# Fused transformer layers with two expert stages: norm of the last layer moved behind the return of the rows, 23 and 29 tiles

## The chip, the cores and the metric

The program runs on one core of a Trainium2 chip. The metric is device time in microseconds (us) of one execution; the median of three runs before the change is 597.67 us (596.51 to 597.98). The core has a matmul engine (TensorE, PE in the rows; PEld is its weight load), VectorE (DVE), ScalarE (ACT), GpSimd (POOL) and SyncE (SP), which run their own instruction queues in order and wait for each other through semaphores. DMA transfers are issued here by SP and by POOL.

## What is computed

Four blocks over x of shape (4, 512, 128), each followed by a layer norm of residual plus block, all in float32. Only the last one is touched by the change, with the tile counts of both expert blocks:

```
x = _layernorm(x + attention_0(x))
x = _layernorm(x + experts_0(x))      # 8 experts, F = 512, SiLU, top 1
x = _layernorm(x + recurrence_1(x))
x = _layernorm(x + experts_1(x))      # 14 experts, F = 256, GELU, top 1
return x

# experts_1
assignments = argmax(x @ router_w)             # one expert for each of the 2048 rows
weights = softmax(x @ router_w)[assignments]
hid = gelu(x @ w1[e] + b1[e]);  y = hid @ w2[e] + b2[e]
out = y[assigned] * weights
# _layernorm(v): (v - mean(v)) / sqrt(var(v) + 1e-5), over the 128 values of a row
```

## The kernel before

The 2048 rows lie as 16 tiles of 128 rows (four batches of four tiles). Each expert stage works in three steps. GpSimd scatters the rows with indirect DMAs into DRAM, one region of 2048 rows for each expert (L519). VectorE works out on the core which region and offset each "slot tile" of 128 rows comes from (`tabulate`, L1193 on), since the counts per expert are data. Then the slot tiles are worked through in a ring of three. The number of slot tiles is fixed at build time: the most that any split of 2048 rows over E experts can need is (2048 + 127 E) // 128, which is 23 for 8 experts and 29 for 14; `slot_tiles` rounds it up to a multiple of the ring, to 24 and 30. A slot tile past the used ones holds zero rows with an index that the scatter drops.

For each slot tile m of the second expert stage:

- SP reads the tile's offset and loads its 128 rows of 130 values (the row, its index, its router weight) from the region (L470, L473).
- TensorE transposes it (L1010), ScalarE copies it out of PSUM (`turned`, L805), TensorE makes the two hidden chunks (L1018), ScalarE applies GELU (`raised`, L812), TensorE makes the result (L1027).
- VectorE fetches the expert's weights, 642 columns, into the ring (L1393), adds bias (`summed`, L1423), forms statistics of the tile before (`spread`, L1413), multiplies by the router weight and adds the residual (L1428), and combines mean and variance of the tile before (`moments`, L1417). The matmuls of a tile wait for its weight copy.
- GpSimd (`outputs`) takes tiles in groups of three (the last two alone): variance plus epsilon (L507), power -0.5 (L510), minus mean (L623), times scale (L627); after group k it sends the three tiles of group k - 2.
- ScalarE (`normed`, L817) applies scale and shift to tile m - 7, in its queue between the copies and GELUs of tiles m and m - 1, and waits for the group's shift there.
- GpSimd sends a normed tile with one indirect DMA straight to the rows of the output (L616). SP waits at the end for all 30.

```
            for m in range(NT1 + NORM_LAG):
                if m < NT1:
                    turned(m)
                if 1 <= m <= NT1:
                    raised(m - 1)
                if m >= NORM_LAG:
                    normed(m - NORM_LAG)
```

The first expert stage has no norm behind it in the tile loop: VectorE adds the bias, GpSimd scatters the tile into the DRAM tensor `returned_0` (L605), and when all have landed SP loads the rows back in token order with four DMAs of 256 KB (L482); VectorE goes on from there (L1472). Its ScalarE code is six tiles written out and a hardware loop over the rest, three tiles an iteration.

## Time and profile before

| what | value |
|---|---|
| runs | 596.51, 597.67, 597.98 us, median 597.67 |
| the profiled execution | 597.33 us, of which its span (first to last instruction) 595.5 us |
| busy of the span | PE 78%, weight load 55%, VectorE 59%, ScalarE 46%, GpSimd 46% |
| last region of the program, from 588.0 us on | no engine busy |

The profiled execution lies 1.8 us above its own span and 0.3 us below the median. The program has five stretches: attention up to about 320 us, first expert stage to 377 us, recurrence to 503 us, second expert stage to 588 us, and the end. The span is cut in 40 slices in the page, of 14.9 us each; the last three show VectorE at 4, 0 and 0 tenths and GpSimd at 7, 7 and 3:

```profile
DVE  2545666767776777667344666475865656484600
POOL 4323255428654573440212455433445645167773
```

### The profile page before, as it was taken

The page shows a single profiled execution, that of the slowest core. Times are in us where ns is not written, and L with a number is a line of the kernel's source. Part 1 is how long each engine was busy: PE and PEld are TensorE (multiplying, and loading weights), DVE is VectorE, ACT ScalarE, POOL GpSimd, SP SyncE. Part 2 cuts the span into 40 slices and gives each one's busy share as a digit, 9 for nine tenths or more (in the row PEclk, how much of TensorE's full clock was granted, in tenths as well). Part 3 has the DMA queues.
Part 4 walks back from the last instruction along what each step waited for, and adds up shares of the span by engine and source line. Part 5 has one row for each costly group of instructions (what it writes and reads, how often), then busy time and mean ns, then how long its engine had stood idle before and what let it go on. Part 6 is the DMA issues. An engine that isn't in the chain of part 4 may idle for free. (4 is left out here: it accounts for less than half of the span.)

```text
span 595.5 us, 9976 instructions
## 1 busy us (share of the span) xinstructions
PE 465.0 (78%) x3101; PEld 327.2 (55%) x3101; DVE 352.9 (59%) x878; ACT 274.3 (46%) x570; POOL 272.3 (46%) x310
## 2 busy tenths in 40 slices
PE   3888999999999999999666999189797962786600
PEld 3465566565666567666443999134554651665500
DVE  2545666767776777667344666475865656484600
ACT  1043556665666565767310555174462210576510
POOL 4323255428654573440212455433445645167773
PEclk9955999999999999999967999679899985698955
DMA  8999999999920000000211320630000001221100
GB/s 325 179 171 171 164 348 187 193 201 185 190 48 14 2 1 2 19 2 1 81 53 40 81 58 21 215 165 0 0 2 0 19 18 36 56 69 36 36 15 0
DMA packets 65171, 50.73 MB, mean 85 GB/s; under 512 B 3110, under 2 KB 63277, under 8 KB 64480
## 3 DMA queue, kind: packets, MB, share of 16 engines
q1 hardware_dynamic: 62368, 45.87, 39.4%
q0 software_dynamic: 2752, 4.24, 2.1%
q8 instruction: 26, 0.43, 0.3%
q14 instruction: 25, 0.20, 0.1%
HBM read 20.37 MB, written 31.15 MB: 87 GB/s over the span
## 5 line engine op out<-in xcount | busy, mean ns | idle before, releaser
L697 ACT ACTIVATE arena<-banks 128x512 f32<-128x512 f32 x128 | 76.4, 597 | 99.1 <-PE banks L900 98.9
L900 PE MATMUL banks<-ca,work 128*128 128x128 f32 x512 | 86.3, 293 | 17.9 <-ACT arena L697 15.5
L690 ACT ACTIVATE work<-banks,nmax 128x512 f32<-128x512 f32 x128 | 80.7, 686 | 14.2 <-DVE nmax L1273 14.0
L900 PEld LDWEIGHTS banks<-ca,work 128*128 128x128 f32 x512 | 56.2, 146 | 55.7 <-issue 44.2
L1273 DVE TENSOR_REDUCE nmax<-banks 128x2 f32<-128x1024 f32 x64 | 78.4, 1224 | 2.2
L884 PE MATMUL banks<-arena 32*128 32x512 f32 (+3 forms) x256 | 63.2, 454 | 0.0
L873 PEld LDWEIGHTS banks<-arena 32*128 32x128 f32 x256 | 43.2, 193 | 34.3 <-issue 23.7
L873 PE MATMUL banks<-arena 32*128 32x128 f32 x256 | 57.4, 305 | 1.5 <-DVE corr L1356 0.9
L1018 PE MATMUL banks<-t,arena 128*128 128x128 f32 x312 | 50.8, 303 | 4.0 <-ACT t L805 2.4
L1261 DVE COPY_PREDICATED banks<-ca,banks 128x256 f32<-128x256 uint32 x64 | 27.3, 426 | 44.7 <-PE banks L873 44.6
L1018 PEld LDWEIGHTS banks<-t,arena 128*128 128x128 f32 x312 | 43.7, 210 | 7.1 <-issue 4.0
L1027 PE MATMUL banks<-arena,work 128*128 128x128 f32 x312 | 46.4, 286 | 0.9 <-ACT work L812 0.6
L879 PE MATMUL banks<-arena 32*128 32x128 f32 (+2 forms) x192 | 46.2, 419 | 0.0
L1073 PE MATMUL banks<-arena 128*128 128x512 f32 x96 | 43.0, 596 | 1.2 <-POOL arena L669 1.2
L736 ACT ACTIVATE work<-banks,arena 128x128 f32<-128x128 f32 x96 | 27.4, 368 | 32.9 <-PE banks L1018 32.9
L1027 PEld LDWEIGHTS banks<-arena,work 128*128 128x128 f32 x312 | 41.5, 201 | 1.6 <-ACT work L812 1.1
L913 PE MATMUL banks<-arena 128*32 128x256 f32 x512 | 40.9, 394 | 0.0
L605 POOL DMA_INDIRECT returned<-work,arena x24 | 24.0, 998 | 33.1 <-DVE work L1406 19.4
L519 POOL DMA_INDIRECT regions<-xc,pos x16 | 16.4, 1026 | 48.7 <-DVE pos L1183 44.9
L884 PEld LDWEIGHTS banks<-arena 32*128 32x128 f32 x256 | 37.6, 194 | 1.3
L572 POOL TENSOR_TENSOR arena<-ca,corr 128x512 f32<-128x512 f32 x32 | 33.1, 1041 | 8.7 <-DVE nmax L1273 7.3
L1393 DVE COPY arena<-arena 128x642 f32 (+1 forms) x54 | 32.6, 603 | 6.6 <-DVE work L1406 4.5
(212 smaller groups left out, 852.6 us busy)
## 6 DMA issues: line engine op xcount, KB each, us to landing
regions<-zeros SPq DMA_DIRECT2D x15, 1040.0 KB, 18.1
regions<-zeros SPq DMA_DIRECT2D x9, 1032.0 KB, 20.3
arena<-wp_in SPq DMA_DIRECT2D x1, 4624.0 KB, 28.3
arena<-wp_in SPq DMA_DIRECT2D x1, 4494.0 KB, 15.9
arena<-ct_in SPq DMA_DIRECT2D x1, 2048.0 KB, 10.3
arena<-regions SPq DMA_DIRECT2D x30, 65.0 KB, 1.8
arena<-cb_in SPq DMA_DIRECT2D x1, 1667.0 KB, 8.2
arena<-regions SPq DMA_DIRECT2D x24, 64.5 KB, 1.9
```

Of the source, the lines that this page charges most:

```text
L572: eng.tensor_tensor(delta[:, i, :, :], A("ident").unsqueeze(1).broadcast_to([P, HG, P]), corr[:, b % 2, i, g * HG:(g + 1) * HG].unsqueeze( ...
L690: eng.activation(prob[:, r, :], bank[r], ACT.Exp, bias=nmax[:, s % 2, jj:jj + 1]).then_inc(s_exp, 1)
L697: eng.activation(probT[:, v % 2, j0 + jj, :, i % 2 * P:(i % 2 + 1) * P], PT.rearrange("p (t q) -> p t q", t=TB), ACT.Copy).then_inc(s_pTs, 1)
L873: return eng.matmul(DA[:, jj * P:(jj + 1) * P], qa[rows, r, g, mine], ka[rows, r, g, mine], start=True, stop=True)
L879: eng.matmul(bank[2 * (s % 2) + jj][:, 0:split], qa[rows, r, g, mine], ka[rows, r, g, 0:split], start=True, stop=True)
L884: eng.matmul(bank[2 * (s % 2) + jj][:, split:S], qb[rows, r, g, mine], kb[rows, r, g, split:S], start=True, stop=True)
L900: mm = eng.transpose(PT[:, t * P:(t + 1) * P], prob[:, 2 * (s % 2) + jj, t * P:(t + 1) * P], ident)
L913: mm = eng.matmul(CTX[HP * j:HP * (j + 1), 2 * P * hh:2 * P * (hh + 1)], vv[:, b % 2, t, h * HP:(h + 1) * HP], probT[:, v % 2, j, t, :], s ...
L1018: mm = eng.matmul(bank[r][:, c * P:(c + 1) * P], wbuf[:, r, c * P:(c + 1) * P], xTs[:, r, :], start=True, stop=True)
L1027: mm = eng.matmul(bank[3 + r][:, 0:D], hT[:, r, c * P:(c + 1) * P], wbuf[:, r, F + c * D:F + (c + 1) * D], start=(c == 0), stop=(c == CH - 1))
L1073: mm = eng.matmul(bank[4 + v % 2], R(name, k * INNER + c * P, P), uu[:, r, k, :], start=(k == 0), stop=(k == NC - 1))
L1273: eng.tensor_reduce(nmax[:, s % 2, :], pair, AX.X, ALU.max, negate=True).then_inc(count(s_fixed), 1)
```

## The change

The tile counts become 23 and 29. In the second expert stage the norm leaves the tile loop. A tile's rows, before the norm, now have mean and variance as two more columns (`moments` writes them beside the row), and GpSimd scatters the 130-wide rows in token order into a new DRAM tensor `returned_1`, with nothing else in its queue. When all 29 have landed, SP loads them back in four DMAs of four tiles. ScalarE takes the root of variance plus epsilon of a batch's four tiles, VectorE the reciprocal and the shift, and the norm is split, two tiles of a batch on VectorE and two on ScalarE; SP stores each pair with a plain DMA, eight in all. A table load for the root (with a dummy root behind it) stands at the end of ScalarE's tile loop. The first stage's ScalarE loop is written out.

```
-NORM_LAG = 7
+BY_DVE = 2
 def slot_tiles(experts):
-    most = (B * S + experts * (P - 1)) // P
-    return -(-most // RING) * RING
+    return (B * S + experts * (P - 1)) // P
...
+    sums = nc.dram_tensor("returned_1", (B * S, DW1), F32, kind="Internal").ap()
-        y1 = arena2[:, 0:NT1 * D].rearrange("p (m d) -> p m d", m=NT1)
+        y1 = arena2[:, 0:NT1 * DW1].rearrange("p (m d) -> p m d", m=NT1)
...
             expert_rows(1, E1, NT1)
-            eng.wait_ge(s_store, 16 * NT1)
+            eng.wait_ge(s_sent, 16 * NT1)
+            for b in range(B):
+                eng.dma_start(xbw[:, b * TB:(b + 1) * TB, :],
+                              sums[b * S:(b + 1) * S, :].rearrange("(t p) d -> p t d", p=P)).then_inc(s_back1[b], 16)
+            for b in range(B):
+                for k, s_half in enumerate((s_fin_v, s_fin_a)):
+                    at = slice(b * TB + k * BY_DVE, (b + 1) * TB if k else b * TB + BY_DVE)
+                    eng.wait_ge(s_half, (b + 1) * (TB - BY_DVE if k else BY_DVE))
+                    eng.dma_start(out_view[:, at, :], xa[:, at, :]).then_inc(s_store, 16)
+            eng.wait_ge(s_store, 2 * 16 * B)
...
+            eng.memset(eps1[:, :], 1e-5).then_inc(s_set, 1)
...
-            def outputs():
...
+            def sums_back():
+                for m in range(NT1):
                     eng.wait_ge(s_xload[1][m % LOADS], 16 * (m // LOADS + 1))
-                    eng.wait_ge(s_norm1, m + 1)
-                    eng.indirect_dma_start(out_rows, bass.IndirectOffsetOnAxis(ap=xt[:, m, D:D + 1].bitcast(I32), axis=0),
+                    eng.wait_ge(s_var1, m + 1)
+                    eng.indirect_dma_start(sums[:, :], bass.IndirectOffsetOnAxis(ap=xt[:, m, D:D + 1].bitcast(I32), axis=0),
                                            y1[:, m, :], None, bounds_check=B * S - 1, oob_is_err=False)\
-                       .then_inc(s_store, 16)
...
-                for m in range(2 * RING):
+                for m in range(nt):
                     tile(m, m % RING, m < RING)
-                with eng.Fori(2, nt // RING) as it:
-                    for r in range(RING):
-                        tile(it * RING + r, r, False)
...
-            for m in range(NT1 + NORM_LAG):
+            for m in range(NT1 + 1):
                 if m < NT1:
                     turned(m)
-                if 1 <= m <= NT1:
+                if m >= 1:
                     raised(m - 1)
-                if m >= NORM_LAG:
-                    normed(m - NORM_LAG)
+            eng.activation(few[:, 0:1], eps1[:, :], ACT.Sqrt).then_inc(s_outa, 1)
+            for b in range(B + 1):
+                if b < B:
+                    eng.wait_ge(s_back1[b], 16)
+                    eng.activation(scale1[:, b * TB:(b + 1) * TB], xbw[:, b * TB:(b + 1) * TB, D + 1], ACT.Sqrt,
+                                   bias=eps1[:, :]).then_inc(s_root, 1)
+                if b >= 1:
+                    eng.wait_ge(s_scale1, 2 * b)
+                    for t in range((b - 1) * TB + BY_DVE, b * TB):
+                        eng.activation(xa[:, t, :], xb[:, t, :], ACT.Identity, bias=shift1[:, t:t + 1],
+                                       scale=scale1[:, t:t + 1]).then_inc(s_fin_a, 1)
...
-                    eng.bn_aggr(mv1[:, m, :], st1[:, m, :]).then_inc(s_var1, 1)
+                    eng.bn_aggr(y1[:, m, D:D + 2], st1[:, m, :]).then_inc(s_var1, 1)
...
             experts(1, NT1, F1, WW1, wp1)
+            for b in range(B):
+                tiles = slice(b * TB, (b + 1) * TB)
+                eng.wait_ge(s_root, b + 1)
+                eng.reciprocal(scale1[:, tiles], scale1[:, tiles]).then_inc(s_scale1, 1)
+                eng.wait_ge(s_scale1, 2 * b + 1)
+                eng.scalar_tensor_tensor(out=shift1[:, tiles], in0=xbw[:, tiles, D], scalar=-1.0, in1=scale1[:, tiles],
+                                         op0=ALU.mult, op1=ALU.mult).then_inc(s_scale1, 1)
+                for t in range(b * TB, b * TB + BY_DVE):
+                    eng.tensor_scalar(xa[:, t, :], xb[:, t, :], xbw[:, t, D:D + 1], scale1[:, t:t + 1],
+                                      ALU.subtract, ALU.mult).then_inc(s_fin_v, 1)
```

How it moves instructions. GpSimd's queue in the second expert stage, before (one group of three tiles and its sends; each such row is one instruction, "x3" three):

```order
L510 TENSOR_TENSOR scale<-scale,half 128x3
L623 TENSOR_SCALAR shift<-mv 128x3
L627 TENSOR_TENSOR shift<-shift,scale 128x3
L616 DMA out<-arena 2048x128 x3
L507 TENSOR_SCALAR scale<-mv 128x1
```

The four small operations of a group stand between the sends of one group and the next. Now, from the last scatters into the regions (L531) to the end of GpSimd's queue:

```order
L531 DMA regions<-xb,pos 30720x130 x4
L519 TENSOR_SCALAR rstda<-mva 128x4
L522 TENSOR_TENSOR rstda<-rstda,half 128x4
L531 DMA regions<-xb,pos 30720x130 x8
L626 DMA returned<-arena 2048x130 x29
L194 UNCONDITIONAL_BRANCH
```

Between the 29 sends nothing is left. ScalarE's queue at the end of the tile loop, before:

```order
L805 ACTIVATE t<-banks 128x128
L812 ACTIVATE work<-banks,arena 128x128 x2
L817 ACTIVATE arena<-arena,shift,scale 128x128
L812 ACTIVATE work<-banks,arena 128x128 x2
L817 ACTIVATE arena<-arena,shift,scale 128x128 x7
L194 UNCONDITIONAL_BRANCH
```

The norm (L817) of an earlier tile stands between the copy and the GELUs of each two tiles. The same place now:

```order
L797 ACTIVATE t<-banks 128x128
L804 ACTIVATE work<-banks,arena 128x128 x4
L813 ACT_TABLE_LOAD
L813 ACTIVATE few<-eps 128x1
L817 ACTIVATE scale<-xb,eps 128x4 x2
L822 ACTIVATE xa<-xb,shift,scale 128x128 x2
L817 ACTIVATE scale<-xb,eps 128x4
L822 ACTIVATE xa<-xb,shift,scale 128x128 x2
L817 ACTIVATE scale<-xb,eps 128x4
L822 ACTIVATE xa<-xb,shift,scale 128x128 x4
L194 UNCONDITIONAL_BRANCH
```

The norm activation between two tiles' GELUs is gone. The root of batch b + 1 stands ahead of the norm of batch b, and no second table load follows.

## Rows read from the trace of the kernel before

**Rows 1.** Waits, 528 to 566 us: who for whom, us in total, times, longest
```profile
ACT arena L817 <- POOL shift L627: 12.5, 6, 3.1
```

**Rows 2.** Timeline, second expert stage, GpSimd: start us, us, engine, line, operation
```profile
540.69 0.19 POOL L507 TENSOR_SCALAR scale<-mv 128x3 f32<-128x3 f32 x1
542.95 1.25 POOL L616 DMA_INDIRECT out<-arena  x1 [0.60 <-ACT arena L817]
544.51 0.98 POOL L616 DMA_INDIRECT out<-arena  x1 [0.30 <-issue]
...
546.84 0.19 POOL L507 TENSOR_SCALAR scale<-mv 128x3 f32<-128x3 f32 x1
```

**Rows 3.** Timeline, the end of the second expert stage, and the waits of SP's queue
```profile
565.02 0.18 DVE L1417 BATCH_NORM_AGGREGATE mv<-st 128x2 f32<-128x6 f32 x1
587.23 0.97 POOL L616 DMA_INDIRECT out<-arena  x1 [0.30 <-issue]
...
SPq L194 <- PEq L194: 6.0, 1, 6.0
```

**Rows 4.** Timeline, VectorE between 516 and 535 us
```profile
516.13 0.18 DVE L1417 BATCH_NORM_AGGREGATE mv<-st 128x2 f32<-128x6 f32 x1
...
517.58 0.46 DVE L1393 COPY arena<-arena 128x642 f32 x1
518.18 0.29 DVE L1423 TENSOR_TENSOR arena<-banks,arena 128x128 f32<-128x128 f32 x1
...
534.64 0.29 DVE L1423 TENSOR_TENSOR arena<-banks,arena 128x128 f32<-128x128 f32 x1
```

**Rows 5.** Timeline, the last hidden matmuls, and SP's loads of slot tiles
```profile
561.74 0.71 PE L1018 MATMUL banks<-t,arena 128*128 128x128 f32 x4 [2.38 <-ACT t L805]
...
506.49 23.93 SPq L473 DMA_DIRECT2D arena<-regions  x22
```

**Rows 6.** The first stage's returns: its sends, then the timeline of its end
```profile
L605 POOL DMA_INDIRECT returned<-work,arena x24: 980/982/1353, 330.5 to 375.1; - x24
...
374.00 0.29 DVE L1406 TENSOR_TENSOR work<-banks,arena 128x128 f32<-128x128 f32 x1 [1.21 <-PE banks L1027]
377.29 2.03 SPq L482 DMA_DIRECT2D xa<-returned  x4
380.21 1.14 DVE L1472 SCALAR_TENSOR_TENSOR xc<-xa,sm,xb 128x128 f32<-128x128 f32 x4 [5.58 <-DMA xa<-returned]
```

**Rows 7.** Windows: us, busy of PE, PEld, DVE, ACT, POOL, granted PE clock, DMA share, GB/s
```profile
328.00:374.00 46.00, 45.62 (x392) 44.80 (x390) 28.60 (x65) 27.52 (x93) 22.37 (x23) 1.00 0.19 52
506.00:513.50 7.50, 4.09 (x16) 3.50 (x17) 0.00 (x0) 3.15 (x8) 0.00 (x0) 0.50 0.20 47
520.00:531.00 11.00, 10.20 (x74) 8.43 (x73) 9.79 (x42) 9.17 (x32) 5.81 (x12) 1.00 0.26 61
```

**Rows 8.** DMAs to landing: SP's loads of returned rows (L482), then issues by kind
```profile
DMA to landing us min/median/max: 2.9/3.9/5.8
...
out<-arena POOLq DMA_INDIRECT x30, 2.2
...
regions<-xb,pos POOLq DMA_INDIRECT x16, 2.3
```

**Rows 9.** Timeline: durations of the kinds that the change adds, and of a table load
```profile
567.02 1.26 ACT L817 ACTIVATE arena<-arena,shift,scale 128x128 f32<-128x128 f32 x3 [3.53 <-POOL shift L627]
...
385.35 1.12 DVE L1464 TENSOR_SCALAR z<-xc,mva,rstda 128x128 f32<-128x128 f32 x4
...
498.37 0.18 DVE L1550 RECIPROCAL xb<-sm 128x4 f32<-128x4 f32 x1
...
510.32 1.28 ACT L812 ACT_TABLE_LOAD   x1
```

**Rows 10.** Timeline: VectorE's bias additions of tiles 0 and 1, at the low clock
```profile
513.55 0.29 DVE L1423 TENSOR_TENSOR arena<-banks,arena 128x128 f32<-128x128 f32 x1 [8.49 <-PE banks L1027]
...
515.47 0.29 DVE L1423 TENSOR_TENSOR arena<-banks,arena 128x128 f32<-128x128 f32 x1 [0.83 <-PE banks L1027]
```

54 lines of the change are left out of this document (19 added, 35 removed).

## Prediction
> **What bounds the kernel now.** I read the timeline of the last hundred microseconds first, then the waits there, then the windows for the clock. Up to the second expert stage nothing but tile counts, a 0.1 us memset and the form of one ScalarE loop changes, so this is where the case is decided. The reader is to see that the stage is not bound by its arithmetic. GpSimd's queue sets the pace: from one group's first small operation to the next group's it is 546.84 - 540.69 = 6.15 us for three tiles, 2.05 us a tile, of which the three sends take 546.84 - 542.95 = 3.9 us and the small operations with the pauses around them the rest [rows 2]. ScalarE stands still for GpSimd's shift, 12.5 us between 528 and 566 us in six waits [rows 1], and since the norm sits in ScalarE's queue ahead of the next tile's copy, TensorE and VectorE stand too. Where GpSimd isn't yet in the way the loop is faster: VectorE's bias additions of tiles 3 and 15 stand at 518.18 and 534.64 us, 16.46 us for 12 tiles, 1.37 us a tile, with VectorE busy 9.79 of 11.0 us in that stretch [rows 4, 7]. And after VectorE's last statistics at 565.20 us the program goes on for 30.3 us of the 595.5 us span: GpSimd works off its backlog until 588.20 us, the last send lands, and 6.0 us of program end follow [rows 3].
>
> **The change, part by part.** All on the time scale of the profiled execution (span 595.5, time 597.33 us).
>
> *First stage, 24 to 23 tiles.* TensorE is busy 45.62 of 46.00 us there and the sends go from 330.5 to 375.1 us in 23 steps, 1.94 us each [rows 6, 7]. One tile less is 1.94 us off the path, since the returns, and all behind them, wait for the last send. Writing out ScalarE's loop: ScalarE is busy 27.5 of 46 us and waits for TensorE; nothing. The memset and the small table instructions (29 in place of 30 columns): nothing, they stand beside DMA waits.
>
> *Second stage, the loop.* Removed: 11 groups of four GpSimd operations, 30 norm activations, one tile. Each engine's load then is: VectorE as before, 1.37 us a tile; GpSimd one send, 1.28 us when one follows another (0.98 and 0.30) [rows 2]; SP one load in 23.93 / 22 = 1.09 us [rows 5]. VectorE becomes the bound, with SP's loads hidden ahead of it and GpSimd just hidden behind it. The start doesn't move (tile 3 at 518.18 us). Tile 26's bias addition comes at 518.18 + 23 x 1.37 = 549.7 us; the copy of the last tile's weights ends 0.14 us before that (it ends at 518.04 ahead of 518.18) [rows 4], at 549.55; the last hidden matmuls wait for it alone, I put 0.1 us; and from these to the end of the last statistics it is 565.20 - 561.74 = 3.46 us [rows 3, 5]. That gives 553.1 us in place of 565.2 us: 12.1 us off.
>
> *Second stage, the tail.* In place of the 30.3 us:
> - Last statistics to SP's first load of the returned rows: the first stage has the same chain, 374.29 to 377.29 us, 3.0 us [rows 6]. It holds only if GpSimd has no backlog.
> - First load issued to landed: 377.29 to 380.21 us, 2.9 us [rows 6].
> - Four batches through ScalarE. The loads there landed 2.9 to 5.8 us after issue, with issues 0.5 us apart, and the last of them shared the DMA engines with the load of the second stage's weights, issued right behind it [rows 8]. So the last lands 1.5 us (the issues alone) to 4.4 us (5.8 + 1.5 - 2.9) after the first; I take 2.7, 0.9 us a load, as there is no weight load here. ScalarE's order is root 0, root 1, norm 0, root 2, norm 1, root 3, norm 2, norm 3. It starts its chain with the second landing, 0.9 us, and then has three roots and eight norm activations; three of these take 1.26 us in a row, 0.42 each [rows 9]; a root of 4 columns I put at 0.3 with its wait (no row has one; between the 0.18 of the reciprocal and a norm's 0.42, both without a wait). Together 0.9 + 0.9 + 3.4 = 5.2, and 0.1 for a wait: 5.3 us. VectorE needs less, 0.2 + 0.2 and two operations of 0.28 a batch [rows 9], beside it. Bounds: 4.8 with landings 0.5 us apart; 6.5 if the last landing comes 4.4 us late and root, reciprocal, shift and four norms follow it.
> - The last store of 128 KB: no row shows a plain store. The scatters of 64 KB land in 2.2 and 2.3 us, the load of 256 KB in 2.9 [rows 8]; I take 2.4 with the issue, between 2.1 and 3.5.
> - The end: 6.0 us [rows 3].
>
> Sum 3.0 + 2.9 + 5.3 + 2.4 + 6.0 = 19.6 us, 10.7 less than 30.3. The table load of 1.28 us [rows 9] stands in ScalarE's queue while the returns travel (5.9 us), so it is hidden; without that cover it would cost its 1.3 us.
>
> Total: 1.9 + 12.1 + 10.7 = 24.7 us off, span 570.8, time 572.6 us in the profiled execution. The median stands 0.34 us above that execution: **573.0 us**.
>
> The returned rows are 520 bytes long in place of 512. What bears on it: scatters of 520-byte rows land in 2.3 us and of 512-byte rows in 2.2 us [rows 8], so I charge nothing. The Trainium skill (DMA: Bandwidth & Descriptors, section How a descriptor splits into AXI transactions) speaks against the change: a descriptor that doesn't start at a multiple of 256 bytes is split into more transactions, 25 beats in place of 18 in its example of 576 bytes. By that rule, an estimate from the page, the loads would be spaced nearer 1.3 than 0.9 us and the sum would be about 574. The rows here show no such difference for scatters, and none shows it for loads.
>
> **The rivals.**
>
> *A, the sends don't keep pace.* In the first stage each send starts 0.84 us after VectorE's result (374.29 to 375.13, "375.1") and takes 0.98 [rows 6]. If each of the 29 sends pays both, 1.82 us, GpSimd is the bound again: from the first statistics (516.31 - 1.94 = 514.4 us) 28 x 1.82 = 51.0 to the start of the last wait and 0.84 to its send, 566.2 us, in place of 551.2 + 0.84 = 552.0. That is 14.2 us more, 587. For it: in the first stage all sends looked like that. Against: a send that is already due follows after 0.30 us, 1.28 us in all, with VectorE busy [rows 2], so one that falls behind catches up. The Trainium skill (GPSIMD Engine Reference, section 1. Specifications) says that GpSimd shares its SBUF interfaces with VectorE and contends with two-input and two-port operations; by that page VectorE's work in the loop would slow the sends, which would feed this rival. The rows speak against that: 0.98 us and 0.30 us before it for a send in the middle of VectorE's work, 0.97 and 0.30 at the end, when VectorE is idle [rows 2, 3].
>
> *B, the clock stays low.* At 506 to 513.5 us TensorE has half clock (0.50, the level of 1.2 GHz) after a long pause, and tiles 0 and 1 are 1.92 us apart; from 520 us it has 1.00 [rows 7, 10]. Should it stay low, 25 tiles x 0.55 = 13.8 us more: 587. Against it: the loop before reaches 1.00 in the same work, and the new loop only has fewer pauses.
>
> *C, slower: the scatters drain one by one.* If the DMA queue of GpSimd takes a scatter of 520-byte rows only when the one before has landed, 29 x 2.3 us [rows 8] from 515.2 us ends at 581.9 us, in place of 554.2 for SP's first load: 27.7 us more, 600.7 us. It decides from 2.26 us a scatter on. Against it: sends are issued 1.28 us apart, each landing in 2.1 to 2.3 us, so two are under way together [rows 2, 8].
>
> *D, the change saves less in the tail*: landings, semaphores and SP's eight store issues at 0.5 us add up to 5 us more than summed, 578.
>
> **How the numbers follow.** Forecast 0.74, D 0.08 (inside the range), A 0.08, B 0.05, C 0.03, something else that leaves the time where it is 0.02. The low end takes 0.3 in place of 0.84 us for the last send, ScalarE's 4.8, the store's 2.1 and a pace of 1.33 us, 0.5 + 0.5 + 0.3 + 1.0 = 2.3 us less, and 1.2 us for the spread of the runs (597.67 to 596.51): 569.5. The high end takes 1.2 for ScalarE, 1.1 for the store and 2.3 for a pace of 1.46, 577.6, or D, and with the spread 579.5. A measurement of this kernel tells 0.3% (1.8 us) from no change. Faster 0.96, same 0.01, slower 0.03.
>
> **What would show it.** Right: no wait of ScalarE for GpSimd in the second stage; VectorE's bias additions 1.37 us apart to the end; last statistics at 551 us; 29 sends about 1.37 us apart with the last starting under 1 us after the last statistics; SP's first load at 554, its landing at 557, the last norm at 562, the last store landed at 565. Wrong: sends 1.8 us apart (A), a granted clock of 0.50 behind 515 us (B), landing times that grow from send to send (C), a table load between root and norm, or over 6 us between the first landing and the last store's issue (D).

## The result, and the profile after

| | before | changed |
|---|---|---|
| median of 4 runs each, beside each other | 597.23 us (596.51 to 597.98) | 564.62 us (558.62 to 567.04) |
| ratio, with its 95% interval | | 0.942 (0.9335 to 0.9505) |
| the profiled execution, its span | 597.33, 595.5 us | 567.04, 565.1 us |
| busy of the span: PE, VectorE, ScalarE, GpSimd | 78, 59, 46, 46% | 81, 63, 47, 44% |

The kernel is 32.6 us faster in the median. The forecast said 24.7 us (573.0 us), and its range went down to 569.5 us, 5 us above the result: right in direction, too small in size. Executions of one kernel lie up to 14 us apart here, the shorter ones with a higher mean granted clock of TensorE (the kernel before, in later runs, 588 to 591 us at 0.902 and above, 596 to 603 us at 0.888 and below), and the ratios here and below leave out the executions over 1.5% above the fastest of their kernel, so they can differ a little from those of the medians.

Where the clock differs is ahead of anything that the change touches. Between 30 and 60 us TensorE is granted 0.50 to 0.53 in eleven of the fourteen profiles of this study and 0.89 to 0.91 in three. The changed kernel's profile (0.51) and that of the kernel with its sends held back (0.91), described below, run the same instructions on VectorE up to the second expert stage's statistics, and reach the first of these at 512.5 and at 503.2 us. Of the 32.6 us some 2 come from this: the kernel before's four executions, 596.5 to 598.0 us, all have the lower clock by their times, the changed kernel's have 566.6 and 567.0 us with the lower one (means 0.902 and 0.905), 562.6 and 558.6 us with a higher one (0.913 and 0.921). With the lower clock in both it is 30 us, and the two profiled executions, 0.52 and 0.51 between 30 and 60 us, are 30.3 us apart.

The profiled run splits at two instants that both kernels have, the first and the last of VectorE's statistics in the second expert stage:

| stretch | before | changed | difference | forecast |
|---|---|---|---|---|
| start of the program to VectorE's first bias addition there | 513.55 | 509.95 | -3.60 | -1.94 |
| first to last statistics | 48.9 | 37.0 | -11.9 | with the tile count -12.1 |
| end of the last statistics to the end of the span | 30.3 | 15.4 | -14.9 | -10.7 |

The loop first. The waits of the changed kernel between 513 and 548 us (who for whom, us in total, times, longest) in place of [rows 1]:

```profile
ACT work L804 <- PE banks L1015: 13.8, 25, 0.9
POOL returned L626 <- DVE arena L1414: 12.7, 1, 12.7
POOL returned L626 <- issue: 9.1, 25, 0.7
...
DVE arena L1420 <- PE banks L1024: 0.5, 1, 0.5
```

ScalarE waits only for TensorE, 0.9 us at the most; no wait of it for GpSimd is left. VectorE waits for TensorE once, 0.5 us. VectorE's timeline at the start of the loop (start us, us, engine, line, operation), to hold against [rows 4, 10]:

```profile
509.95 0.29 DVE L1420 TENSOR_TENSOR arena<-banks,arena 128x128 f32<-128x128 f32 x1 [8.45 <-PE banks L1024]
511.87 0.29 DVE L1420 TENSOR_TENSOR arena<-banks,arena 128x128 f32<-128x128 f32 x1 [0.84 <-PE banks L1024]
513.23 0.29 DVE L1420 TENSOR_TENSOR arena<-banks,arena 128x128 f32<-128x128 f32 x1
514.58 0.29 DVE L1420 TENSOR_TENSOR arena<-banks,arena 128x128 f32<-128x128 f32 x1
515.94 0.29 DVE L1420 TENSOR_TENSOR arena<-banks,arena 128x128 f32<-128x128 f32 x1
```

From the second tile on they stand 1.35 to 1.36 us apart (two later steps take 1.54 and 1.71), without an idle gap here, so VectorE is the bound, as forecast (1.37). The windows (us, busy of PE, PEld, DVE, ACT, POOL, granted PE clock, DMA share, GB/s), to hold against [rows 7], show full clock, but don't decide the bound: VectorE is busy 28.26 of 32 us and TensorE 28.41. What decides it is who waits, and the run with the bias on TensorE below.

```profile
240.00:320.00 80.00, 63.53 (x484) 41.11 (x480) 44.96 (x110) 37.42 (x63) 22.29 (x28) 0.94 0.09 31
...
516.00:548.00 32.00, 28.41 (x207) 23.77 (x208) 28.26 (x117) 19.18 (x69) 23.38 (x24) 1.00 0.29 71
```

The first line bears on the other 1.66 us of the start: over the same 80 us of attention, which the change doesn't touch, this execution has a granted clock of 0.94 and the one before 0.89. The experiments come back to it.

Then the end. Timeline of the changed kernel from the third last statistics on, in place of [rows 3]:

```profile
548.11 0.17 DVE L1414 BATCH_NORM_AGGREGATE arena<-st 128x2 f32<-128x6 f32 x1
...
549.08 0.17 DVE L1414 BATCH_NORM_AGGREGATE arena<-st 128x2 f32<-128x6 f32 x1
...
549.42 0.98 POOL L626 DMA_INDIRECT returned<-arena  x1 [0.38 <-DVE arena L1414]
549.53 0.18 DVE L1414 BATCH_NORM_AGGREGATE arena<-st 128x2 f32<-128x6 f32 x1
550.70 0.98 POOL L626 DMA_INDIRECT returned<-arena  x1 [0.30 <-issue]
551.98 0.98 POOL L626 DMA_INDIRECT returned<-arena  x1 [0.30 <-issue]
554.14 2.03 SPq L491 DMA_DIRECT2D xb<-returned  x4
557.08 0.30 ACT L817 ACTIVATE scale<-xb,eps 128x4 f32<-128x4 f32 x1 [7.95 <-DMA xb<-returned]
...
558.33 4.98 SPq L497 DMA_DIRECT2D out<-xa  x8
...
560.90 1.63 ACT L822 ACTIVATE xa<-xb,shift,scale 128x128 f32<-128x128 f32 x4
```

And what SP waits for last, with the drain of GpSimd's queue that ends a program (duration in ns three times, first and last start):

```profile
L194 POOLq DRAIN  x1: 9428/9428/9428, 550.5 to 550.5; - x1
```

```profile
SPq L194 <- DMA out<-xa: 1.4, 1, 1.4
```

The wait of 6.0 us at the program's end [rows 3] has gone; 0.2 us of it is left. In the kernel before, GpSimd's drain stands at 585.5 us:

```profile
L194 POOLq DRAIN  x1: 9757/9757/9757, 585.5 to 585.5; - x1
```

It ends at 585.5 + 9.76 = 595.3 us, the end of the program and 8.1 us after the last send's start at 587.23. In the changed kernel it ends at 550.5 + 9.43 = 559.9 us, 7.9 us after 551.98, but now 5 us ahead of the end, beside loads and norms. That is an observation on two traces; the experiments ask whether it is the cause.

### The profile page after: what moved, and what is told of

Same layout as the page of the kernel before. It is cut to its first block and busy times, and to the rows that moved or that the text cites. A ratio compares the mean times of both kernels' runs of the same rounds, so it can differ in the third digit from the quotient of the medians.

```text
span 565.1 us, 9780 instructions
## 1 busy us (share of the span) xinstructions
PE 457.9 (81%) x3075; PEld 319.9 (57%) x3075; DVE 354.3 (63%) x886; ACT 266.6 (47%) x547; POOL 250.3 (44%) x261
## 5 line engine op out<-in xcount | busy, mean ns | idle before, releaser
L897 PE MATMUL banks<-ca,work 128*128 128x128 f32 x512 | 86.5, 294 | 17.9 <-ACT arena L692 15.5
L1015 PE MATMUL banks<-t,arena 128*128 128x128 f32 x300 | 47.6, 297 | 3.7 <-ACT t L797 1.0
L876 PE MATMUL banks<-arena 32*128 32x128 f32 (+2 forms) x192 | 46.3, 420 | 0.0
L1015 PEld LDWEIGHTS banks<-t,arena 128*128 128x128 f32 x300 | 40.7, 205 | 8.7 <-issue 7.2
L1024 PE MATMUL banks<-arena,work 128*128 128x128 f32 x300 | 43.4, 281 | 0.9 <-ACT work L804 0.5
L731 ACT ACTIVATE work<-banks,arena 128x128 f32<-128x128 f32 x92 | 26.2, 368 | 32.2 <-PE banks L1015 31.1
L1024 PEld LDWEIGHTS banks<-arena,work 128*128 128x128 f32 x300 | 38.8, 197 | 1.5 <-ACT work L804 1.0
L626 POOL DMA_INDIRECT returned<-arena x29 | 29.4, 1012 | 22.7 <-DVE arena L1414 13.0
L531 POOL DMA_INDIRECT regions<-xc,pos x16 | 16.4, 1024 | 48.1 <-issue 30.2
L617 POOL DMA_INDIRECT returned<-work,arena x23 | 22.6, 983 | 32.5 <-DVE work L1403 30.9
## 6 DMA issues: line engine op xcount, KB each, us to landing
arena<-wp_in SPq DMA_DIRECT2D x1, 4494.0 KB, 15.4
```

Of the source, the lines that this page charges most:

```text
L876: eng.matmul(bank[2 * (s % 2) + jj][:, 0:split], qa[rows, r, g, mine], ka[rows, r, g, 0:split], start=True, stop=True)
L897: mm = eng.transpose(PT[:, t * P:(t + 1) * P], prob[:, 2 * (s % 2) + jj, t * P:(t + 1) * P], ident)
L1015: mm = eng.matmul(bank[r][:, c * P:(c + 1) * P], wbuf[:, r, c * P:(c + 1) * P], xTs[:, r, :], start=True, stop=True)
L1024: mm = eng.matmul(bank[3 + r][:, 0:D], hT[:, r, c * P:(c + 1) * P], wbuf[:, r, F + c * D:F + (c + 1) * D], start=(c == 0), stop=(c == CH - 1))
```

## The experiments

They ran in four groups, each on a chip of its own; kernels of one group share their runs of the kernel before.

### The drain

The changed kernel once more, unaltered:

> The changed kernel once more, for its spread. Four runs so far lie between 558.6 and 567.0 us, far wider than the 1.5 us of the kernel before, and its profiled run reached tile 3 of the second expert stage 3.60 us earlier than before where one tile of the first stage accounts for 1.94. Theory N (the rest is the granted TensorE clock between 240 and 330 us, 0.94 against 0.89, which changes from run to run): the median of five comes out within 2 us of 564.6, and in the new profile the 1.6 us are of another size or gone. Theory L (the rest comes with the written-out ScalarE loop or another layout in memory): tile 3 comes 3.6 us earlier than before again, within 0.3 us.

The tile counts and ScalarE's written-out loop alone; statistics, norm and sends as in the kernel before:

```diff
 def slot_tiles(experts):
-    most = (B * S + experts * (P - 1)) // P
-    return -(-most // RING) * RING
+    return (B * S + experts * (P - 1)) // P
```

> The kernel before with 23 and 29 tiles and the first stage's ScalarE loop written out, the norm where it was. Theory N: 1.94 us off in the first stage and 2.05 us (GpSimd's pace of a tile) in the second, 593.2 us against 597.2. Theory L: 1.6 us more than that off, 591.6. In both the end of the program comes 8.0 us after GpSimd's last send starts, 6.0 us after that send has landed.

The norm behind the returns alone, with the rounding to 24 and 30 tiles and ScalarE's loop kept:

> The changed kernel with 24 and 30 tiles and the hardware loop on ScalarE in the first stage, so only the norm moved. Theory N: 1.94 us and one tile of the new pace, 1.36 us, more than the changed kernel: 567.9 us where that has 564.6. Theory L: 1.6 us more again, 569.5. Bias additions of the second stage 1.36 us apart in both, and the last send 2.3 us behind the last statistics, since the last three statistics come faster (0.97 and 0.46 us apart) than sends can follow (1.28).

The changed kernel with one more send at the very end, to rows that nobody reads:

```diff
             eng.wait_ge(s_store, 2 * 16 * B)
+            eng.wait_ge(s_spare, 16)
 ...
+                eng.wait_ge(s_fin_v, B * BY_DVE)
+                eng.indirect_dma_start(spare[:, :], bass.IndirectOffsetOnAxis(ap=xt[:, 0, D:D + 1].bitcast(I32), axis=0),
+                                       y1[:, 0, :], None, bounds_check=B * S - 1, oob_is_err=False)\
+                   .then_inc(s_spare, 16)
```

> The changed kernel plus one more indirect send on GpSimd, of tile 0's rows into a spare DRAM tensor, once VectorE has done its last norm (about 561.9 us in the profiled run); SP waits for its landing too. Theory G (the 6.0 us after the last landing in the kernel before were GpSimd's drain, which ends 8.0 us after its last send starts, and the change hid it by sending early): last send starts about 562.8, the drain ends at 570.8 and the span with it, 5.8 us more than the changed kernel. Rival H (the 6.0 us belonged to the end of that program in some other way, such as more instructions or semaphores to leave): the send lands by 565.0 us, about when the last store does, and the time goes up by under 0.5 us.

Measured, beside 596.79 us before:

| kernel | median us | ratio, 95% interval | span of its profile |
|---|---|---|---|
| changed, again | 571.12 | 0.9629 (0.9533 to 0.9725) | 574.7 |
| tile counts alone | 591.02 | 0.994 (0.9876 to 1.0005) | 581.5 |
| norm behind the returns alone | 581.29 | 0.9822 (0.9752 to 0.9892) | 581.1 |
| changed, with a late send | 583.64 | 0.9873 (0.9829 to 0.9918) | 584.1 |

The late send decides. Its timeline, waits of SP and drain:

```profile
565.09 0.98 POOL L629 DMA_INDIRECT returned<-arena  x1 [0.30 <-issue]
...
575.89 0.98 POOL L633 DMA_INDIRECT spare<-arena  x1 [9.83 <-DVE xa L1571]
```

```profile
SPq L195 <- PEq L195: 5.5, 1, 5.5
```

```profile
L195 POOLq DRAIN  x1: 8223/8223/8223, 575.7 to 575.7; - x1
```

All rows of the output are computed by then, the stores are about to land (the changed kernel's program ends 2.6 us behind its last norm), and still the program ends at 584.1 us, 8.2 us after the spare send's start; the drain ends at 575.7 + 8.22 = 583.9. From the last statistics to the end it takes 21.3 us, where the changed kernel beside it takes 15.2: 6.1 us more, with theory G's 5.8 and against rival H's 0.5. The wait of the old end is back with 5.5 us. So the 6.0 us in the kernel before were no fixed end of every program but the rest of GpSimd's drain behind its last indirect send. The drain ends 7.9 to 8.1 us after the start of the last send in all fourteen profiles of this study, both kernels' own among them, wherever that send stands. With the tile counts alone, where GpSimd still sends last, the end is 8.1 us after the last send (573.36 to 581.5) and SP's wait is 5.8 us; with the norm behind the returns alone it is 0.2 us. That part of the gain therefore comes with the norm's new place, not with the tile counts.

How the gain splits between the two parts this group shows only roughly. The tile counts alone are 5.8 us under the kernel before in the median, with an interval that reaches 1; among the executions with the higher clock it is 585.3 us in the median beside 588.8, 3.5 us for the theory's 4. The first to the last statistics take 47.7 us there, the old pace of 1.7 us. The norm behind the returns alone is 15.5 us under it, and 13 us above both of its theories (567.9 and 569.5), with a loop of 49.8 us that has the pauses described below.

The run of the changed kernel brought something neither theory had: 46.3 us from first to last statistics in place of 37.0. More on that below, under the pauses. Of what it asked, the start of the second stage, it says this: the first bias addition comes at 511.0 us here and at 510.0, 512.6 and 511.5 us in the changed kernel's other three profiles, and at 513.6 and 512.2 us in the two of the kernel before. Executions of one kernel differ there by as much as the 1.66 us beyond the one tile, so nothing shows these to be an effect of the change, and theory L's 3.6 us again didn't come (2.6). Theory N's median within 2 us of 564.6 didn't either (571.1), for the pauses.

### Sends beside the loop, and the bound of the loop

This chip showed no pauses. The kernel before and the changed one once more:

> The kernel before once more, for its profile on the chip of the runs beside it. In the last set the changed kernel's second stage took 46.3 us from the first to the last statistics where the run shown with the result took 37.0, with pauses of 1.3 to 2 us about every 5 to 6 us in which VectorE and ScalarE stand and go on within 0.03 us of each other. Theory S (slack): the kernel before has such pauses too, but its loop waits for GpSimd anyway, so they cost it little: first to last statistics within 1.5 us of the 48.9 shown. Rival C (changed code): the pauses come only with the changed kernel, and the kernel before shows no stretch in which VectorE and ScalarE resume together other than behind GpSimd's shift.

> The changed kernel a third time. If the pauses belong to the chip or to the execution, their number here tells: none and the second stage takes 37.0 us from first to last statistics, or as in the last set some six and it takes 45 to 46. The tail is the same in both: last send 2.3 us behind the last statistics, first load 2.2 us behind it, first root 2.9 us later, end of span 15.4 us behind the last statistics.

All 29 sends held back until the last statistics:

```diff
             def sums_back():
+                eng.wait_ge(s_var1, NT1)
```

> The changed kernel with all 29 sends held back until the last statistics are done. Theory P (the sends have a part in the pauses: they write while the loop reads): without sends in the loop no pauses, first to last statistics 37.0 us or less. Rival Q (they belong to TensorE's work, its clock or the loads): the pauses are there as before. In both, 29 sends back to back take 29 x 1.28 = 37.1 us behind the last statistics, about 35 us more than the changed kernel in the same state.

The bias addition given to TensorE, as one more matmul of the bank's sum, and taken from VectorE:

```diff
-                        eng.wait_ge(s_yb[l], m - (RING - 1))
+                        eng.wait_ge((s_yb[0], s_sum1)[l], m - (RING - 1))
+                    if l:
+                        eng.matmul(bank[3 + r][:, 0:D], ident, wbuf[:, r, 2 * F + CH:2 * F + CH + D], start=True, stop=False)
 ...
-                    eng.tensor_tensor(y1[:, m, 0:D], bank[3 + m % RING][:, 0:D], wbuf[:, m % RING, 2 * F + F // P:width],
-                                      ALU.add).then_inc(s_yb[1], 1)
 ...
-                    eng.scalar_tensor_tensor(out=y1[:, m, 0:D], in0=y1[:, m, 0:D], scalar=xt[:, m, D + 1:D + 2],
+                    eng.scalar_tensor_tensor(out=y1[:, m, 0:D], in0=bank[3 + m % RING][:, 0:D], scalar=xt[:, m, D + 1:D + 2],
```

> The changed kernel with the second stage's bias added by TensorE (one more matmul of the identity with the bias columns, 0.11 us) and VectorE reading PSUM once in place of twice (0.21 us less a tile). Theory V (VectorE sets the pace of 1.36 us): where no pauses stand, the pace falls to that of GpSimd's sends, 1.28 us, and the last send starts 2 to 2.6 us earlier behind the first statistics. Rival T (TensorE and the round trip between the engines set it): the pace stays at 1.36 or rises by the 0.11 us of the matmul.

Measured, beside 595.75 us before:

| kernel | median us | ratio, 95% interval | first to last statistics | from there to the end |
|---|---|---|---|---|
| before, again | 596.90 | 1.0049 (0.9993 to 1.0106) | 50.4 | 29.8 |
| changed, a third time | 568.49 | 0.9394 (0.9318 to 0.947) | 37.0 | 15.1 |
| sends held back | 596.97 (592.0 to 601.91) | | 37.0 | 49.8 |
| bias on TensorE | 560.92 | 0.9388 (0.933 to 0.9446) | 34.5 | 15.1 |

The third run of the changed kernel repeats the split of the first within 0.4 us (37.0 and 15.1 against 37.0 and 15.4), so both terms stand. Its six times are 557.0, 561.0 and 568.4 to 570.0 us, the first two with a mean granted clock of 0.92 to 0.93 and the others with 0.90. The ratios of the second and the last line are equal although the medians are 7.6 us apart, because their executions mix the clocks differently; what the bias brings is read from the stretches.

With the sends held back VectorE's loop takes its 37.0 us as ever, and the 28 steps between sends take 36.0 us afterwards:

```profile
540.24 0.18 DVE L1415 BATCH_NORM_AGGREGATE arena<-st 128x2 f32<-128x6 f32 x1
541.21 0.99 POOL L627 DMA_INDIRECT returned<-arena  x1 [49.64 <-DVE arena L1415]
...
577.15 0.98 POOL L627 DMA_INDIRECT returned<-arena  x1 [0.30 <-issue]
```

(577.15 - 541.21) / 28 = 1.28 us, with VectorE idle. The stretch behind the last statistics is 34.7 us longer than the changed kernel's, for an expected 35; the medians are only 28.5 us apart, as the four and six executions mix the clocks differently. Two things follow. The sends cost nothing while they run beside the loop, and they don't slow VectorE: its loop is no faster when GpSimd is silent. And 1.28 us a send is GpSimd's own pace, 0.08 us under VectorE's. What the run was made for, whether the sends have a part in the pauses, it can't say, as no kernel had them on this chip.

The bias on TensorE brings 37.0 - 34.5 = 2.5 us and not 29 times the 0.28 us of the operation taken from VectorE, 8 us. VectorE waits for no send in this loop, so GpSimd can't be what holds its statistics back. TensorE is; its waits, timeline and windows:

```profile
DVE st L1413 <- PE banks L1026: 5.9, 22, 0.6
```

```profile
520.41 0.39 PE L1024 MATMUL banks<-arena,ca 128*128 128x128 f32 x2
520.63 0.61 PE L1026 MATMUL banks<-arena,work 128*128 128x128 f32 x4
```

```profile
514.00:541.00 27.00, 26.89 (x235) 26.29 (x234) 21.44 (x86) 19.09 (x64) 20.57 (x21) 1.00 0.32 82
```

TensorE is busy 26.89 of 27 us, and VectorE waits for it at 22 tiles; the statistics come 1.23 and 1.28 us apart in turn. The added matmul is listed as two and takes 0.22 us (520.41 to 520.63), where 0.11 was expected. So theory V names the bound before (the pace falls from 1.36 us), and rival T's TensorE is the one right behind it. GpSimd is as near: the sends run from 511.5 to 547.5 us, 28 steps of 1.286 us with none but their own 0.3 us between, and the last starts 2.3 us behind the last statistics, as in the changed kernel, so all of the 2.5 us arrive at the end.

### What the tile counts are worth, and what bounds the tail

The changed kernel a fourth time:

> The changed kernel once more, unaltered, as the partner of the next two on the same chip. Theory (differences between its executions come from the start, by the clock that TensorE is granted in 30 to 60 us): times fall on two levels, about 557 to 561 and about 567 to 570 us, and behind the loop's first statistics everything is as before: 36.9 to 37.0 us from the first statistics of the second expert layer to the last, 15.2 to 15.4 us from there to the end of the span. Rival (the loop itself varies, as in the run that took 571.1 us): 45 to 46 us from first to last statistics, with gaps in which VectorE and ScalarE stop together, and times of 570 us and more.

The norm behind the returns alone, again:

```diff
+    most = (B * S + experts * (P - 1)) // P
+    return -(-most // RING) * RING
 ...
-                for m in range(nt):
+                for m in range(2 * RING):
                     tile(m, m % RING, m < RING)
+                with eng.Fori(2, nt // RING) as it:
+                    for r in range(RING):
+                        tile(it * RING + r, r, False)
```

> The root, reciprocal and norm behind the returns alone; the arena's tiles stay 24 and 30 and ScalarE's loop keeps its form. Theory: what the tile counts are worth is one tile of the first layer (1.94 us) and one of the second (1.36 us), so this kernel takes 3.3 us more than the changed kernel beside it (about 568 where that has 564.6), with the last statistics about 38.3 us behind the first ones. Rival (ScalarE's loop, written out by the step, brings something by itself): 4.9 us more than the changed kernel, with 1.6 us more ahead of the second layer's first bias addition than the one tile explains.

The bias on TensorE, and three of a batch's four tiles normed by VectorE:

```diff
-BY_DVE = 2
+BY_DVE = 3
```

> The changed kernel with its bias additions on TensorE (as in the earlier run of that form: 34.6 us from first to last statistics, 15.2 us from there to the end) and with three instead of two of each batch's four tiles normed by VectorE. Theory (ScalarE's chain of roots and norms bounds the stretch behind the last landing): ScalarE has one norm less in each batch, the last norm ends 0.5 to 0.9 us earlier after the last statistics, and the stretch to the end of the span falls from 15.2 to 14.3 to 14.7 us. Rival (the landings of SP's loads and its eight store issues of 0.6 us each bound it): the stretch stays at 15.1 to 15.3 us and the norms only end earlier ahead of stores that wait their turn. What falls the other way: VectorE's third norm comes later than ScalarE's second would have, and the stretch grows by up to 0.5 us.

Measured, beside 597.67 us before (588.91 to 602.89):

| kernel | median us | ratio, 95% interval | first to last statistics | from there to the end |
|---|---|---|---|---|
| changed, fourth time | 568.94 | 0.9634 (0.9574 to 0.9693) | 47.0 | 15.0 |
| norm behind the returns alone | 582.10 | 0.9828 (0.9748 to 0.9907) | 50.5 | 15.0 |
| bias on TensorE, 3 of 4 on VectorE | 575.38 | 0.9662 (0.9579 to 0.9744) | 47.9 | 14.8 |

This chip has the pauses, so the rival on the first kernel held here: 47.0 us, as in the first group. For the bound of the tail the stretch behind the last statistics is clean of them. It came out at 14.8 us, in the gap between the theory's 14.3 to 14.7 and the rival's 15.1. The timeline:

```profile
575.50 0.30 ACT L817 ACTIVATE scale<-xb,eps 128x4 f32<-128x4 f32 x1
...
576.42 0.85 DVE L1564 TENSOR_SCALAR xa<-xb,scale 128x128 f32<-128x128 f32 x3
576.54 0.49 ACT L822 ACTIVATE xa<-xb,shift,scale 128x128 f32<-128x128 f32 x1 [0.35 <-DVE shift L1561]
```

ScalarE is done at 577.03 and VectorE at 577.27 us: both halves now end together, 4.95 us after the first root, where the kernel with the bias on TensorE and two of four takes 5.06 and the changed kernel's profile 5.45. No gain of the new balance is shown: with two of four on VectorE the stretch takes 14.8 to 15.4 us in eight profiles (14.8 with the norm behind the returns alone, first group), so 14.8 lies within what executions differ by. And the bias on TensorE, which took 2.5 us off the loop on the chip before, brings nothing on this one: 47.9 us beside 47.0. Its median is 6.4 us higher, most of which is the clock (three of its six executions have a mean of 0.92, five of the changed kernel's); among those with 0.92 it takes 569.2 to 571.4 us beside 568.2 to 570.3. No version of this study is shown to beat the changed kernel on every chip.

The tile counts are not settled by this. The kernel without them takes 13.2 us more in the median, and 584.0 - 575.6 = 8.4 us more in the profile, where the theory gave 3.3 and the rival 4.9. Of the 8.4 us the first stage has 2.0 (24 sends from 331.5 to 376.1 against 23 from 331.2 to 373.8; the forecast's 1.94), the loop 3.5 (one tile of 1.36 and 2.1 us more of pauses), and 2.7 lie between the stages: from the first stage's last send to the first statistics of the second it has 142.2 us and the changed kernel beside it 139.5, where ten of the other profiles have 140.4 to 141.4. In the first group the medians of the same pair lay 10.2 us apart. So the two tiles themselves are seen with their 3.3 us. The difference of the medians is in good part the clock: of the six executions the kernel without the counts has one with a mean granted clock of 0.917 (574.9 us) and five with 0.894 to 0.903 (579.5 to 585.8), the changed kernel five with 0.918 to 0.921 (568.2 to 570.3) and one with 0.900 (577.5). At like clocks they are some 5 to 6 us apart, and the first group's executions of the kernel without the counts all have the lower clock too. What is left beyond 3.3 us has no cause shown; that the loop of ScalarE, written out by the step, has a part in it is possible and was not tried alone.

### The pauses

On the chips of the first and the third group the second expert stage takes 9 to 13 us more than elsewhere: 46.3 and 47.0 us for the changed kernel's 37.0 from first to last statistics, 45.6 with the late send, 49.8 and 50.5 us with 30 tiles, 47.9 for 34.5 with the bias on TensorE. The timeline of the changed kernel, fourth time:

```profile
517.04 0.97 POOL L626 DMA_INDIRECT returned<-arena  x1 [0.34 <-issue]
...
517.21 0.61 PE L1024 MATMUL banks<-arena,work 128*128 128x128 f32 x4
518.60 0.29 DVE L1420 TENSOR_TENSOR arena<-banks,arena 128x128 f32<-128x128 f32 x1 [2.01 <-PE banks L1024]
518.63 0.28 ACT L797 ACTIVATE t<-banks 128x128 f32<-128x128 f32 x1 [1.62 <-remote]
...
524.51 0.29 DVE L1420 TENSOR_TENSOR arena<-banks,arena 128x128 f32<-128x128 f32 x1 [1.98 <-PE banks L1024]
524.54 0.28 ACT L797 ACTIVATE t<-banks 128x128 f32<-128x128 f32 x1 [1.55 <-PE banks L1007]
```

VectorE and ScalarE, both waiting for TensorE, resume 0.03 us apart, 1.3 to 2.0 us late; in the first of these pauses no compute engine starts anything for about 1 us (up to 518.60). The bias additions with over 1 us of idle time ahead of them are those of these tiles, counted from one:

| kernel | group | tiles |
|---|---|---|
| changed, again | first | 5, 8, 14, 17, 20, 25 |
| norm behind the returns alone | first | 5, 11, 14, 17, 20, 24, 27 |
| changed, with a late send | first | 5, 8, 11, 15, 18, 25 |
| changed, fourth time | third | 5, 8, 12, 15, 21, 25 |
| norm behind the returns alone, again | third | 5, 8, 11, 14, 17, 20, 26 |
| bias on TensorE, 3 of 4 on VectorE | third | 5, 8, 11, 14, 17, 20, 23, 26 |

They come at every third or fourth tile, at nearly the same ones in all six. As the loops also start alike and keep nearly the same pace, this doesn't tell a place in the program from a time since the loop began; a time since the start of the program it isn't, since the loops start up to 5 us apart. The last row is the tile whose result VectorE waits for, as that kernel has no bias addition; TensorE has six matmuls a tile there in place of five, and the tiles are the same, which speaks against a count of TensorE's own instructions.

TensorE isn't alone in it. SyncE stands too, in register instructions that wait for no engine. Their durations (ns, least, median, longest) in the changed kernel, fourth time, and below it in the third, without pauses:

```profile
L475 SPq MOVE arena<-regions x52: 3/29/693, 321.2 to 541.7; - x52
```

```profile
L475 SPq MOVE arena<-regions x52: 29/29/29, 322.8 to 537.3; - x52
```

All seven profiles of the first and the third group have such moves of 0.39 to 0.71 us at the longest, also in the first expert stage, and the other seven none over 0.03 us. The kernel with the tile counts alone is one of the first seven (0.39 us), though its first fifteen statistics stand 1.35 to 1.36 us apart with one step of 1.55, without a pause at tile 5, 8, 11 or 14. So the disturbance of these two chips isn't TensorE's alone, and it is there without the new norm too. Records of 3 ns, a tenth of what the same instruction takes elsewhere, stand beside the long ones, so the recording of the instructions may have a part in it; nothing here tells.

What it costs the comparison can be said. With the higher clock the kernel before takes 588 to 591 us on all three chips, pauses or not; the changed kernel takes 557.0 and 561.0 us on the chip without them and, with a mean of 0.918 and more, 567.5 to 570.3 us on the two with them. The change is worth 27 to 31 us there and about 20 us here.

To ask whether the place is one in TensorE's own program or the number of the tile in its ring of three, I put 14 small matmuls ahead of TensorE's program, meant as one and a half tiles:

```diff
                     transpose(m)
+                    if l == 1 and m == 0:
+                        for _ in range(14):
+                            eng.matmul(bank[0][:, 0:8], ident, ca[:, 0:8], start=True, stop=True)
```

> The changed kernel with 14 small matmuls (8 columns, into a bank that is overwritten behind them) put on TensorE behind the second layer's first transposition, so that everything that follows stands about one and a half tiles later in TensorE's own program, while rings, tiles and data stay. It asks what the pauses hang on that some runs show, in which VectorE and ScalarE, both waiting for TensorE, resume within 0.03 us of each other 1.3 to 2.0 us late: on three kernels and two chips VectorE's late bias additions were those of the 5th, 8th, 11th or 12th, 14th or 15th, 17th, 20th or 21st tile. Theory (they hang on a place in TensorE's program, such as the loading of its instructions): they move one or two tiles forward, to the 4th or 3rd, 6th or 7th, 9th or 10th and so on. Rival (they hang on the rings of three buffers and so on the tile's number): still 5, 8, 11. If this chip is one without pauses, 36.9 to 37.0 us from first to last statistics and nothing is told apart. The 14 matmuls themselves may cost 0 to 2.5 us at the start of the loop.

It took 571.06 us beside 592.29 before (ratio 0.9545, 0.9436 to 0.9653), and its chip has no pauses: 37.0 us from first to last statistics, 15.3 from there to the end. The question stays open. The run wouldn't have told much on a chip with pauses either: a tile has nine listed matmuls (one to transpose, four hidden, four for the result), so 28 listed ones are about three tiles and not one and a half, the very distance at which the pauses follow each other. One price was missed too: the 14 matmuls, listed as 28, took 5.98 us at the low clock and put off the loop's start by about 4 us, where 0 to 2.5 were expected.

```profile
505.44 5.98 PE L1033 MATMUL banks<-ca 128*128 128x8 f32 x28
```

The kernel before itself was not profiled on the chips with pauses.

## Why the prediction was right in direction and wrong in size

The profiled run beats the forecast for it (572.6 us) by 5.6 us, and the median lies another 2.4 us under the profiled run. These 2.4 us and the 0.34 us that the forecast added for the median are the clock of the start, and 1.7 us are an earlier start of the second stage, both luck. They aren't why the range was missed: the profiled run, with the lower clock, lies under it too (567.0), and would with the start where it was (568.7). By its own steps:

- **"The end: 6.0 us [rows 3]" is the step that failed.** It carried a wait of the old end into the new sum as if it came with every end of program. Measured: 0.2 us, and 1.4 us for the last store's landing, which the sum had in a term of its own. It was what remained of GpSimd's drain, 8.1 us from the last send's start, after the 2.1 us that the last rows took to land. Once the sends end 13 us before the program does, it is hidden whole. The late send brings it back (5.5 us). The row itself said whom SP waited for but not for what; the drain of GpSimd's queue, on the same line of the same trace, did, and wasn't read.
- **"Last statistics to SP's first load", 3.0 us, measured 4.43.** The step said "it holds only if GpSimd has no backlog", and then left the backlog out. VectorE's last two statistics come 0.97 and 0.45 us after their predecessors, while sends need 1.28 each, so the last starts 2.27 us after the last statistics and not 0.84. The other half of the term holds exactly: 551.98 to 554.14 us is 2.16, in the first stage 375.13 to 377.29 is 2.16. These 1.4 us go the other way and hid a quarter of the first error.
- **First stage, one tile, 1.94 us: right.** It is 2.0 us between the profiles with 23 and 24 sends. The second stage starts 3.60 us earlier in all; the rest has a higher granted clock in attention beside it and is no more than executions of one kernel differ by.
- **The loop: right.** Pace 1.36 for 1.37 us; 37.0 us from first to last statistics; VectorE the bound, full clock, no wait of ScalarE for GpSimd. TensorE stood just behind VectorE, which the sum didn't say: with 0.28 us less on VectorE it is the bound at 1.26 us. Last statistics at 549.7 us where the summed 551.2 minus the earlier start (1.66) is 549.5.
- **The tail's middle: right.** First landing 2.94 for 2.9 us, roots and norms 5.45 for 5.3, last store 562.53 to 565.1 us, 2.6 for 2.4. The table load stood hidden, and none came between root and norm:

```profile
547.64 1.28 ACT L813 ACT_TABLE_LOAD   x1
```

The tail sums to 4.43 + 2.94 + 5.45 + 2.57 = 15.4 us for 19.6. With the drain alone put right, the forecast had been 567; with the backlog too, 568.5.

The rivals: *A* (sends of 1.82 us) fell. About half of the 0.84 us between a result and its send are spent beside the previous send; in the loop the sends start 1.36 us apart, and back to back 1.28. Against the contention that the GPSIMD Engine Reference of the Trainium skill, section 1. Specifications, would have here: a send beside VectorE's work takes 1.02 us in the median and 0.98 with VectorE idle, 0.04 us, of no weight. *B* (a low clock) fell in this run: 1.00 from 516 us on. *C* (scatters one by one) fell; SP's load went out 2.16 us after the last send's start, and 2.15 with all sends held back. Its limit of 2.26 us a scatter was miscounted: by its own terms (554.2 - 515.2) / 29 = 1.34 us. *D* fell: the landings cost nothing beyond the sum. The rule on split descriptors (the Trainium skill, DMA: Bandwidth & Descriptors, section How a descriptor splits into AXI transactions) shows little at 520-byte rows: the loads land in 4.0 us in the median, those of 512-byte rows in the same profile in 3.7. No rival held the case that came, a fixed-looking cost that goes.

The range was too narrow on the low side for two reasons: the end's 6.0 us had no lower bound in it, though its cause wasn't known, and the spread was taken from three runs (1.5 us) that happened to lie on one level, where runs of one kernel elsewhere lie 9 us and more apart.

## What to carry to other kernels

A wait at the end of a program is somebody's work: before it goes into the sum as fixed, name the engine and the instruction that ends it (here GpSimd's drain, 8 us from its last indirect send), and ask whether the change moves that instruction off the end. At the end of a pipelined loop the last items come faster than the pace; the slower queue behind it adds its backlog, and that belongs in the sum. And three runs that agree within 0.3% say little on a kernel whose executions differ in the clock: compare medians only among executions with like clocks; the split by stretches (first to last statistics, from there to the end) repeated within 0.4 us on chips without pauses while the medians moved by 4.

## What the runs showed of the hardware that was not expected

- GpSimd's drain at the end of a program ends 7.9 to 8.1 us after the start of its last indirect send, in fourteen profiles, wherever in the program that send stands.
- Two profiles with the same work up to the second expert stage reach its first statistics 9.3 us apart, with a clock granted to TensorE between 30 and 60 us of 0.51 (the changed kernel) and 0.91 (the held-back sends).
- On the chips of two of the four groups VectorE and ScalarE got TensorE's results 1.3 to 2.0 us late at every third or fourth tile of the second expert stage, at nearly the same tiles on both; 9 to 13 us in all. Single register instructions of SyncE took up to 0.7 us there, and 0.03 us on the other chips. The changed kernel's ratio was 0.963 there and 0.939 to 0.942 on chips without it (0.9545 with the 14 matmuls added). The cause is open.
- 14 matmuls of 8 columns cost TensorE 6 us at half clock, 0.43 us each.
